# Attention tiles that are scored a second time in turned form instead of being transposed

## The reference

```python
h = relu(layernorm(x))
q, k, v = split(h @ W_qkv + b_qkv)           # 8 heads of 16 columns
scores = where(adj, q @ k.T * 0.25, -inf)    # 512 x 512 for each head, adj symmetric, diagonal set
x = x + (softmax(scores) @ v) @ W_out + b_out
h = relu(layernorm(x))
z_l, z_g, vv = h @ Wl, h @ Wg, h @ Wv
A_l = relu(cosine(z_l, z_l)); A_g = exp(-|z_g - z_g'|^2 / 2)   # zero diagonal, masked by adj
K = 0.9 * A_l / rowsum(A_l) + 0.1 * A_g / rowsum(A_g)
x = x + (K @ vv) @ Wo
```

## Time and profile before

| | |
|---|---|
| median of three runs | 953.59 us |
| span of the profiled execution (first to last instruction) | 952.0 us |
| TensorE matmuls | 869.2 us busy, 91% |
| VectorE | 800.4 us, 84% |
| ScalarE | 686.6 us, 72% |
| GpSimd | 189.4 us, 20% |
| mean granted TensorE clock | 0.993 of 2.4 GHz |

### The profile page before, as it was taken

The page is one execution under the profiler, slowest core; times in us unless marked ns, Lnnn a source line. Parts: engine busy times, 40 slices in busy tenths (PEclk is TensorE's granted clock), DMA queues, the critical chain, the costliest instruction groups (busy, mean ns, idle before and its releaser), DMA issues.

```text
span 952.0 us, 21653 instructions
## 1 busy us (share of the span) xinstructions
PE 869.2 (91%) x6067; PEld 612.4 (64%) x6067; DVE 800.4 (84%) x2460; ACT 686.6 (72%) x1185; POOL 189.4 (20%) x270
## 2 busy tenths in 40 slices
PE   2688999999999999999999999999999999999977
PEld 1454658576685857667585766758576675858565
DVE  2777889798988989898898989899898989979765
ACT  1387877787877777787777778777877878787721
POOL 1221222131212213121221312122131221211110
PEclk9899999999999999999999999999999999999999
DMA  2321212121111212111111211111121111110000
GB/s 66 94 78 51 62 34 67 57 67 33 56 55 33 66 55 66 33 55 55 36 63 55 66 36 52 55 42 59 54 66 39 50 55 51 62 35 1 12 12 12
DMA packets 62423, 47.56 MB, mean 50 GB/s; under 512 B 7600, under 2 KB 62384, under 8 KB 62384
## 3 DMA queue, kind: packets, MB, share of 16 engines
q1 hardware_dynamic: 62384, 47.09, 16.3%
HBM read 30.28 MB, written 16.78 MB: 49 GB/s over the span
## 4 chain that ended last, share of the span: by engine, by line
PE 74%; DVE 6%; issue 5%; ACT 4%; DVEq 0%; POOL 0%; ACTq 0%; POOLq 0%
PE turn L545 18%; PE pv L557 13%; PE adj L572 12%; PE adj L566 11%; PE score L535 11%; PE work L579 5%; ACT probs L919 2%; PE work L566 2%; PE work L657 2%; PE work L642 1%; DVE bn_sb L729 1%; DVE resid L861 1%; DVE masked L764 1%; ACT probs_t L912 1%; ACT col_term L964 1%
## 5 line engine op out<-in xcount | busy, mean ns | idle before, releaser
L919 ACT ACTIVATE probs<-masked,neg_max 128x512 f32<-128x512 f32 x512 | 368.6, 727 | 154.6 <-DVE neg_max L764 149.1
L764 DVE CUSTOM_DVE_ANT_0 masked<-score,mask_add 128x512 f32<-128x512 f32 x512 | 344.2, 685 | 35.3 <-PE score L535 33.8
L545 PE MATMUL turn<-ident,probs 128*128 128x128 f32 x2048 | 311.5, 274 | 3.5 <-ACT probs_t L912 2.0
L545 PEld LDWEIGHTS turn<-ident,probs 128*128 128x128 f32 x2048 | 253.4, 141 | 53.2 <-issue 9.7
L912 ACT COPY probs_t<-turn 128x512 f32<-128x512 f32 x384 | 222.4, 579 | 23.6 <-PE turn L545 23.1
L535 PE MATMUL score<-qk_rows 96*128 96x512 bf16 x512 | 198.4, 388 | 12.0 <-DVE neg_max L764 11.0
L557 PE MATMUL pv<-probs_t,v_cols 128*32 128x512 f32 x1024 | 135.7, 604 | 0.4 <-issue 0.4
L535 PEld LDWEIGHTS score<-qk_rows 96*128 96x128 bf16 x512 | 49.9, 98 | 109.5 <-DVE neg_max L764 59.1
L772 DVE COPY probs_t<-turn 128x512 f32<-128x512 f32 x128 | 87.8, 686 | 0.0
L572 PE MATMUL adj<-z,adj_cos 128*128 128x130 f32 x512 | 67.8, 276 | 1.5 <-DVE adj_cos L780 0.8
L572 PE MATMUL adj<-z,adj_rbf 128*128 128x130 f32 x512 | 67.3, 275 | 0.0
(11 more groups left out here) (101 smaller groups left out, 1025.2 us busy)
## 6 DMA issues: line engine op xcount, KB each, us to landing
qk_rows<-split_dram SPq DMA_DIRECT2D x384, 64.0 KB, 2.3
split_dram<-split SPq DMA_DIRECT2D x32, 384.0 KB, 2.6
x_sb<-in_x_dram SPq DMA_DIRECT2D x16, 256.0 KB, 2.9
out_dram<-out_sb SPq DMA_DIRECT2D x16, 256.0 KB, 2.3
masked<-in_adj_dram SPq DMA_DIRECT2D x1, 256.0 KB, 3.4
wqkv_sb<-in_L_gnn_W_qkv_dram SPq DMA_DIRECT2D x1, 192.0 KB, 2.6
bias_v<-in_L_gnn_b_qkv_dram SPq DMA_DIRECT2D x1, 64.0 KB, 3.1
bias_out<-in_L_gnn_b_out_dram SPq DMA_DIRECT2D x1, 64.0 KB, 3.8
```

Of the source, the lines that this page charges most:

```text
L545: last = pe.transpose(turn_bank[u % 2][:, j * P:(j + 1) * P], probs[:, u % 4, j * P:(j + 1) * P], ident[:, :])
L764: dve.tensor_tensor_reduce(masked[:, u % 4, :], score_bank[u % 2][:, :], mask_add[:, u % T, :], -SCALE, 3.0e38, ALU.add, ALU.min, neg_max[ ...
L919: act.activation(probs[:, u % 4, :], masked[:, u % 4, :], ACT.Exp, bias=neg_max[:, u:u + 1], scale=-1.0).then_inc(probs_ready.sem, 1)
```

## The change

**Tiles.** The exponential no longer starts from the tile that VectorE masked. VectorE still adds the mask to each score tile and reduces the row maximum, but its tile goes to `scrap`, which nobody reads. When the 16 maxima columns of half a batch are there, VectorE splits them into three bf16 parts (`max_split`, four short instructions), TensorE transposes them (`max_turn`), ScalarE copies them, and three DMAs of SP lay them as rows 96 to 98 beside the 96 rows of q; the k side has ones in these rows. TensorE then computes each tile again with k as the stationary and q as the moving operand, 99 rows, 21 slots (`LAG`) after the first product of the same number: this gives the turned scores minus the maxima, in PSUM. ScalarE takes the exponential from there straight into `probs_t`. Tiles are now taken in sets of four heads for one block of keys.

**Mask.** For 24 tiles of 32 GpSimd multiplies the exponential's bits by 0 or 1 as int32, in place, one slot after ScalarE. For each fourth tile (`MASK_BY_PE`) TensorE first adds a tile of 0 or -2^100 by a bf16 product with the identity. The transposes, all 32 copies of a batch from PSUM, and the tile's `masked` and `probs` buffers are gone.

**Order.** The loop is written out as straight code (`slots`). The table counts slots from the batch's first score tile. Taken modulo 32, the second half of the layer (z, cos, rbf, mix, norms) is moved by 16 slots against the score tiles, `hT`, q and k stay at 3, 6 and 8, and `pv` stands in every fourth slot (28, 0, 4, ..., 24). `ln_rstd` stays in slot 5 and `ln_scale` in slot 2. `qk_rows` is double-buffered, v is written straight to one of three `v_cols`, and GpSimd's three copies (L455, L471, L483) are gone. In the setup, VectorE also casts the turned mask to int32 and makes the barrier tile, and GpSimd writes ones to the 32 lower rows of `qk_rows`.

The diff, cut to its core:

```diff
-TURN_LAG = 3
-VECTOR_UNITS = (3, 5, 6, 17, 21, 22, 27, 28)
+SLOTS = 32
+LAG = 21
+MASK_BY_PE = (3,)
 AT = {
...
+    "ln_moments": (-32,), "ln_scale": (-30,), "hT": (-29,), "hT_split": (-28,), "ln_rstd": (-27,),
+    "q": (-26,), "k": (-24,), "qk_store": (-22,), "rows0": (-18,), "x_biased": (-16,), "x_next": (-14,),
+    "v": (-12,), "rows1": (-11,),
+    "max_split": (16, 32), "max_turn": (17, 33),
+    "pv": (28, 32, 36, 40, 44, 48, 52, 56), "pv_copy": (41, 57), "y": (44, 59), "yT": (60,), "attn": (62,),
+    "ln2_moments": (63,), "ln2_rstd": (63,), "ln2_scale": (66,), "h2T": (68,), "z": (70, 71, 72, 73),
+    "z_sums": (74,), "zgT": (74,), "zgT_read": (75,), "z_norms": (76,), "col": (78,), "zlT": (79,),
+    "rbf": (81, 83, 89, 93), "rbf_exp": (82, 84, 90, 93), "rbf_mask": (84, 86, 92, 95),
+    "cos": (82, 89, 92, 94), "mix_cos": (95, 96, 100, 102), "mix_rbf": (96, 98, 100, 102), "store": (103,),
+}
+FIRST, LAST = -32, 104
...
+    def due(slot, name):
+        for nth, at in enumerate(AT[name]):
+            batch, rest = divmod(slot - at, SLOTS)
+            if rest == 0 and 0 <= batch < B:
+                return batch, nth
+        return None
+    def tile_due(slot, lag):
+        batch, u = divmod(slot - lag, SLOTS)
+        return (batch, u) if 0 <= batch < B else None
+    slots = range(FIRST, LAST + SLOTS * (B - 1))
...
         @block.sync
...
+                if hit := due(s, "max_turn"):
+                    b, g = hit
+                    reached(sp, max_copied, b, g + 1)
...
+                    for part in range(3):
+                        sp.dma_start(
+                            qk_rows[ROWS + part:ROWS + part + 1, b % 2, 0, g * HG:(g + 1) * HG, :],
+                            max_rows[part * HALF:(part + 1) * HALF, g, :]).then_inc(max_loaded[g].sem, 16)
...
         @block.gpsimd
...
+            for s in slots:
+                if hit := tile_due(s, LAG + 1):
+                    b, w = hit
+                    if w in by_pool:
...
+                        reached(pool, probs_ready, b, w + 1)
+                        tile = probs_t[:, w // HG % 4, w % HG, :].bitcast(I32)
+                        pool.tensor_tensor(tile, tile, keep_t[:, w // HG % T, :],
+                                           ALU.mult).then_inc(probs_masked.sem, 1)
...
+                if hit := due(s, "ln_rstd"):
...
+                for which, name in enumerate(("q", "k")):
...
+                if hit := due(s, "z_norms"):
...
         @block.tensor
...
-                reached(pe, masked_ready, batch, u - 1)
...
-            def turn(batch, u):
-                reached(pe, probs_ready, batch, u + 1)
...
-                for j in range(T):
-                    last = pe.transpose(turn_bank[u % 2][:, j * P:(j + 1) * P],
-                                        probs[:, u % 4, j * P:(j + 1) * P], ident[:, :])
-                last.then_inc(turned.sem, 1)
+                reached(pe, max_ready, b, u - 1)
...
+            def turned_scores(b, w):
+                g, k = divmod(w, HALF)
+                j, hl = divmod(k, HG)
+                h = g * HG + hl
+                if k == 0:
+                    reached(pe, max_loaded[g], b)
+                reached(pe, probs_ready, b, w - 1)
+                if w in by_pe:
+                    pe.matmul(turned_bank[w % 2][:, :], ident_b[:, :], bar_t[:, j, :], start=True, stop=False)
+                pe.matmul(turned_bank[w % 2][:, :], qk_rows[0:ROWS + 3, b % 2, 1, h, j * P:(j + 1) * P],
+                          qk_rows[0:ROWS + 3, b % 2, 0, h, :], start=w not in by_pe,
+                          stop=True).then_inc(turned_filled.sem, 1)
...
         @block.vector
...
+                    dve.tensor_tensor_reduce(scrap[:, u % 2, :], score_bank[u % 2][:, :], mask_add[:, u % T, :], -1.0,
+                                             3.0e38, ALU.add, ALU.min,
+                                             neg_max[:, u // HALF, u % HALF:u % HALF + 1]
+                                             ).then_inc(max_ready.sem, 1)
+                if hit := due(s, "max_split"):
...
+                    dve.tensor_copy(max_parts[:, g, 0, :], neg_max[:, g, :]).then_inc(max_hi.sem, 1)
...
+                    dve.tensor_tensor(max_rest[:, :], neg_max[:, g, :], max_parts[:, g, 0, :],
+                                      ALU.subtract).then_inc(max_rest_ready.sem, 1)
...
         @block.scalar
...
-                        act.activation(probs[:, u % 4, :], masked[:, u % 4, :], ACT.Exp,
-                                       bias=neg_max[:, u:u + 1], scale=-1.0).then_inc(probs_ready.sem, 1)
...
+                    act.activation(probs_t[:, k % 4, w % HG, :], turned_bank[w % 2][:, :], ACT.Exp,
+                                   scale=SCALE).then_inc(probs_ready.sem, 1)
```

More of the change, by code:

```diff
@@ L23 @@
 BF16 = mybir.dt.bfloat16
+I32 = mybir.dt.int32
 ALU = mybir.AluOpType
@@ L324, in work_bank_free @@
-        def work_bank_free(engine, i, use):
-            at = [name for name, _, _, _ in WORK_USES].index(use)
-            for back in range(1, len(WORK_USES) + 1):
-                _, sig, nth, offset = WORK_USES[(at - back) % len(WORK_USES)]
-                batch = i + offset - (1 if back > at else 0)
-                if isinstance(batch, int) and not 0 <= batch < B:
-                    continue
-                reached(engine, sig, batch, nth)
-                return
+        WORK_TURNS = sorted(
+            (AT[name][nth] + SLOTS * b, order, name, nth, b)
+            for b in range(B)
+            for order, (name, nth) in enumerate((
+                ("max_turn", 0), ("max_turn", 1), ("hT", 0), ("q", 0), ("k", 0), ("v", 0), ("y", 0), ("y", 1),
+                ("yT", 0), ("attn", 0), ("h2T", 0), ("zgT", 0), ("col", 0), ("zlT", 0))))
@@ new lines, in graph_blocks, with work_bank_free @@
+        WORK_DONE = {
+            ("max_turn", 0): (max_copied, 1), ("max_turn", 1): (max_copied, 2), ("hT", 0): (hT_ready, 1),
+            ("q", 0): (rest_ready, 1), ("k", 0): (rest_ready, 2), ("v", 0): (v_ready, 1), ("y", 0): (y_ready, 1),
+            ("y", 1): (y_ready, 2), ("yT", 0): (yT_ready, 1), ("attn", 0): (x1_ready, 1),
+            ("h2T", 0): (h2T_split, 1), ("zgT", 0): (zgT_split, 1), ("col", 0): (col_ready, 1),
+            ("zlT", 0): (zlT_split, 1),
+        }
+        def work_bank_free(engine, batch, name, nth=0):
+            place = [turn[2:] for turn in WORK_TURNS].index((name, nth, batch))
+            if place:
+                _, _, name, nth, batch = WORK_TURNS[place - 1]
+                sig, count = WORK_DONE[name, nth]
+                reached(engine, sig, batch, count)
@@ L563, in split_product @@
             def split_product(dst, left, right):
[L565 to L566 removed]
+                for part, (a, c) in enumerate(((0, 0), (0, 1), (1, 0))):
+                    last = pe.matmul(dst, left(a), right(c), start=(part == 0), stop=(part == 2))
                 return last
```

1008 lines of the change are left out of this document (499 added, 509 removed).

## The result

The changed kernel takes 1104.53 us (median of four runs, 1101.02 to 1105.67), the kernel before beside it 953.38. The ratio is 1.157, with an interval of 1.156 to 1.159. The forecast was 961 and its range ended at 1003. The direction, slower, had been given a chance of 0.54; the size was wrong.

The account below looks back on a forecast made before the run. It took TensorE and VectorE to be nearly full and tied by two-bank handovers. Beginning 38.4, batches 29, 38, 52, 12 x 56.7 and 47, end 75 gave 959.8, plus 1.6: 961 us, range 895 to 1003.

Parts of the forecast that it names:

- Part 3: VectorE's work in slots 9 to 31, 0 and 1: rows sum to 33.4 us, plus 3.0 kept waits, 36.4.
- Part 1: TensorE from `hT` (slot 3) to the end of the k product (slot 8): crowded work summing to 11.9 us.
- The balance of loads: Busy sums per batch: TensorE 46, VectorE 45.9, GpSimd 40.6, ScalarE 29.5 us; balance alone would give a 51.6 us period.
- The ring: The steady cycle followed from `hT` to the next batch's `hT`, six pieces summing to a period of 56.7 us.
- parts 5 and 6: `ln_rstd` behind a GpSimd product, 4.2 us with VectorE waiting 2.5; then `ln_scale` 1.0 us before `hT`.
- Part 2: ScalarE and VectorE read k: one activation, one VectorE pass and handovers, 1.7 us.
- Parts 3 to 5: VectorE's slots 36.4 us, detour at the norms behind GpSimd 1.5, detour at `ln_rstd` 4.2.
- Part 6: `ln_scale` on VectorE, after which `hT` can start: 1.0 us.
- the shared path to the memory: Rival, slower: GpSimd slows VectorE's maskings and sums of squares by 1.5 us a batch; period 58.2, total 979; chance 0.07.
- blocked outright: Harsher figure of the shared memory path rival, VectorE fully stopped beside GpSimd: total 1010 us.
- Detours hide: Rival, faster: GpSimd's norm and root steps come in time, period 52.7, total 907 us; chance 0.30.
- only the loads count: Rival, faster: the deeper lag overlaps engines so well that the period is 50, total 875 us; chance 0.10.

Follow-up runs that it names:

- e1: The change with all 32 masks of a batch added by TensorE and no products on GpSimd; 989.8 us, ratio 1.037.
- e10: The change with 16 products instead of 24, the next batch's chain moved to chosen later slots, sums of squares on ScalarE; 956.5 us, ratio 1.004.
- e6: The change with only the next batch's chain (moments, norm, hT, q, k, v) moved 10 slots later, all 24 products kept; 1012.7 us, ratio 1.062.

## Why the prediction was wrong

**The step that failed.** Part 3 took VectorE's rows from a kernel whose GpSimd is idle ("sums of squares 1.7; splits 1.5") and kept them beside 24 products; they and one mask took 6.2 us more in a batch. Part 1 took TensorE's work at full clock behind a gap; it took 2.4 us more. Over batches 3 to 14 these two make up the 97 us of the table within some 6, and the 97 are two thirds of the 143.

**The balance of loads** held for GpSimd (40.6 against 40.4), the product (1.285 against 1.296), ScalarE (29.5 against 28.3; the exponential from PSUM took 0.60 where 0.65 was taken, but the 29.5 is the sum at the old 0.73, and at 0.65 it would have been some 27, so that this agreement is in part luck). For VectorE it failed by the holds: 45.9 against 51.9.

**The ring**, from `hT` at 589.04 to `hT` at 654.06, part by part. *Part 1*, `hT` to the end of the k product, was 11.9 and took 14.4 (the copy of k starts at 603.40). The work was counted rightly; 2.4 of the 2.5 us is the half clock behind the gap (5.27 for what should be 0.44 + 0.66 + 1.79 = 2.9). The prediction priced all of TensorE's work at full clock and forecast gaps of that kind itself, by its waits in parts 5 and 6; no step joined the two. *Part 2*: 1.7 against 1.5. *Parts 3 to 5* were 42.1 in sum and took 48.0 (604.93 to 652.89). The waits were right: VectorE idles 6.3 us there in the waits that its timeline names, 2.33 of it for the root, where 3.0 + 1.5 + 2.5 = 7.0 was forecast. The failed term is "sums of squares 1.7; splits 1.5": four held sums cost 4.1 more, two held casts 1.7 more, one `adj_rbf` 0.4 more, 6.2 in all. *Part 6*: 1.0 against 1.2. Together 65.0 where 56.7 stood.

**The rival that came true** is the shared path to the memory, given 0.07. It was underpriced twice. Half of the common time was taken from one row (0.28 us common, 0.14 lost). A held sum ends 0.14 to 0.18 us behind the product though it takes 0.28, so some 0.1 us of an instruction passes during its wait; with that, the row of before can be read as a whole hold too (of 0.28 us common, 0.28 less 0.1 would be lost, and 0.14 was), and the rival's "blocked outright" was the form nearer to the truth. And it was applied to 4.2 us of instructions in a batch, in proportion to GpSimd's busy share. A lock does not work in proportion: what counts is how many short instructions meet a product, each paying up to 1.28 us whatever its size, so that a cast of 0.17 us pays most. It also left out the norms, which read one tile, and the splits, which read 16 columns. Even outright it was priced at 1010, since nothing followed from it in TensorE's clock.

**The sum of the causes** cannot be split without remainder, as they feed each other. By removal, one at a time: products without their large inputs -91 us, all products off GpSimd -115, the chain moved -92, gaps filled -36. On the kernel before, by addition: large inputs +102, powers in GpSimd's order +16.

**The ends.** The first three batches were forecast by one engine's sum each and took 31 us more (150 against 119). In e1, without products, they took 38.2, 40.2 and 53.9, or 13 us more than forecast, so 18 of the 31 went with the products; e10, with 16 products, other places and the sums on ScalarE, had 36.0, 41.4 and 48.8. What the 13 are was not tried. After the last tile 85.6 against 75; in e1 80.5. Some 5 us of it are the products; what the rest is was not tried.

**The chances.** "Detours hide" (0.30) and "only the loads count" (0.10) had rested on the depth of 21 slots. It does cover exponentials and products: the matmuls of `pv` wait 0.6 us for them in the whole run. It covers nothing of the next batch's chain, whose steps follow each other within a few slots.

## What to carry to other kernels

Before work is given to an idle GpSimd, list VectorE's instructions that go from SBUF to SBUF or read two tiles there, and price each meeting with a large GpSimd instruction at what is left of that instruction, up to its whole length, for short ones too. Not all of them are held (the row statistics were not), so look for a row of each kind. Leave VectorE the work that reads PSUM, or give ScalarE the rest. And a gap of TensorE of some microseconds should be priced twice: itself, and the half clock of what follows.

## What the runs showed that was not expected

- A GpSimd product or sum of 128x512 (1.28 us) holds VectorE's sum of squares, f32 norm step, two-tile mask and even a cast of 16 columns until it ends (0.17 to 1.29 us). Score tiles, which read PSUM and one tile, stayed at 681 to 685 ns in every kernel. The row statistics of the norm, one tile from SBUF, kept their 0.86 us from 582.02 on beside a product (581.17 to 582.43); one step of four took 278 ns at the median and 285 at most in the 50 that ran beside products.
- GpSimd pays in turn: in e6 a product that met a running `adj_rbf` of VectorE took 1.73 us, and three took 4.21 us, against 3.86.
- An int32 product costs GpSimd what an f32 sum costs: 1296 and 1285 ns.
- Up to 128 useless matmuls a batch made the kernel 36 us faster.
